# Products whose result nobody reads, put on TensorE before its first transposition and in four idle places

## The chip, the cores and the metric
One NeuronCore of one Trainium2 chip runs the kernel. The metric is the device time of one execution in microseconds (us), the median of several runs. Other executions than the profiled one carry no trace; durations below come from that single profiled execution.

## The reference, cut to what matters
The input x is 16 batches of 256 tokens of 128 features, float32. Two residual layers follow each other.

```
x = x + attention(layernorm(x))       # 16 heads, 16 query/key features, 8 value features a head
    q, k, v = x @ Wq, x @ Wk, x @ Wv;  q = q / 4
    A = (q . k)^2 under a causal mask;  o = (A v) / (sum of A + 1e-5);  o @ Wo
    # chunked in the reference with a running state; equal to one causal pass over 256 tokens
x = x + moe(layernorm(x))             # 8 experts, the last chosen of the best 2 writes the token
    scores = softmax(x @ gate_w + gate_b);  best two;  wi = score of the expert
    y = relu(x * wi @ w1[e] + b1[e]) @ w2[e] + b2[e]        # 128 -> 512 -> 128
```

Where both of a token's two experts write, the later one stands, so each token needs one expert only, and the kernel sorts tokens by that expert.

## The kernel before, in words
**Attention.** The work goes batch by batch, 16 batches, in `PERIODS`: in period p the scores belong to batch p-1, while projections of the next batch and the tail of earlier ones are laid between them. A batch's scores are made in four groups of four heads (`score_group(b, g)`, into the four banks of `sc`). ScalarE squares a group (`square`, line 416), which also frees `sc` for the next group; GpSimd masks it (`mask`, line 566); TensorE multiplies it by the values (`weigh`, into `av`). VectorE transposes and divides (`spread`, `divide`), TensorE applies Wo (`project_o`), VectorE adds the residual (`residual`) and chooses the expert (`route_*`). GpSimd sends each token's row to its expert's region in memory (`scatter`, line 594).

**Experts.** 39 tiles of 128 rows. For each tile TensorE runs `go_up` (eight recorded instructions into `sc`), a transposition of a later tile (`transpose_xw`), and `go_down` of the tile before (into `av` for even tiles, `p5` for odd ones). ScalarE makes the lower half of relu (`relu_low`, line 516), VectorE the upper half (`relu_high`, line 997) and the sum with the bias (`end_y`, line 1009). In the first ten tiles VectorE also works off `late_piece(t)`: the residual, the second normalisation and the routing of the last batches.

**Order.** Every engine's order is written out by hand; engines wait for one another by semaphores and run their own list strictly in order. On TensorE's list the start is: wait for `dve_const`, `transpose_xn(0)`, `centre_gate`, the first halves of the K and Q projections (`project_half`), `gate_output`, the second K half, and then `first_period`, which begins with `score_group(0, 0)`. The second K half waits for `half_k_ready[1]`, VectorE's copy of the first half (line 705). VectorE reaches that copy only after it has cleared `v_ext` (lines 685 to 692). GpSimd's constants come first of all: `ones` is one of its memsets (line 544), and `pool_step` becomes 1 with the iota of line 549. After the last period TensorE's list is: transposition of the biases, `project_o(14)`, `weigh(15, 2)`, the table load `experts(pe, 0)`, `weigh(15, 3)`, `transpose_xw(0)` and `(1)`, `go_up(0)`, `project_o(15)`, `transpose_xw(2)`, `go_up(1)`, `transpose_xw(3)`, `go_down(0)`, `prefix(6)`, `go_up(2)`.

All of TensorE's products are recorded under the helper's line 1068, transpositions under 1071. A float32 product is recorded as two instructions, a bfloat16 one as one.

Of the kernel before, what the change touches and what calls it, by code (L numbers as in the profile page):

```python
# [7 lines left out]
def after(engine, semaphore, count):  # L8

    if not (isinstance(count, int) and count <= 0):  # L10
        engine.wait_ge(semaphore, count)


def attention_moe_kernel(nc, x, Wq, Wk, Wv, Wo, gate_w, gate_b, w1, b1, w2, b2, out):
# [7 lines left out]
    NB, L, D = x.shape  # L22
    P = 128
    NTK = L // P
    H, F, HD = 16, 16, 8
    E, _, FF = w1.shape
# [49 lines left out]
    with ctx:  # L76
        def sb(name, shape, dt=fp32):
            return ctx.enter_context(nc.sbuf_tensor(name, shape, dt))

        def sem(name):  # L80
            return ctx.enter_context(nc.semaphore(name))
# [17 lines left out]
        ones = sb("ones", [P, P], bf16)  # L99
# [87 lines left out]
        sc = ctx.enter_context(nc.psum_tensor("sc", [P, GH, 512], fp32))  # L187
        av, p5, p6, p7 = [ctx.enter_context(nc.psum_tensor(n, [P, 512], fp32)) for n in ("av", "p5", "p6", "p7")]
# [16 lines left out]
        pool_step = sem("pool_step")  # L205
# [72 lines left out]
        def of(p, lag):  # L278
            return p - lag if 0 <= p - lag < NB else None

        def pair_of(p, lag):

            return (p - lag) // PAIR if 0 <= p - lag < NB and (p - lag) % PAIR == 0 else None
# [16 lines left out]
        def experts(engine, w):  # L300

            engine.wait_ge(table_ready[w], 1)
            words = loaded(engine, expert_i[w][0:1, :], E ** PACK - 1)
            return [(words[t // PACK] >> (BITS * (t % PACK))) & (E - 1) for t in range(LENGTH[w])]
# [761 lines left out]
        def _(pe):  # L1066
            def mm(o, l, r, start=True, stop=True):
                return nc.tensor.matmul(o, lhsT=l, rhs=r, start=start, stop=stop)  # L1068

            def transpose(o, i):  # L1070
                return nc.tensor.transpose(o, i, ident[:, :])  # L1071

            def score_group(b, g):


                if b == 0 and g == 0:
                    pe.wait_ge(half_q_ready, 1)
                if b == 0 and g < 2:
                    pe.wait_ge(half_k_ready[g], 1)
                if g == (2 if b == 0 else 0):  # L1080
                    pe.wait_ge(q_ready, b + 1)
                if b == 0 and g >= 2 or b > 0 and g < 2:
                    pe.wait_ge(k_ready[g % 2], b + 1)
                after(pe, squared, GROUPS * b + g)
                q, k, at = q_sb[b % 2], k_sb[b % 2][g % 2], (g // 2) * L
                for c in range(GH):
                    strip = slice(STRIP * c, STRIP * (c + 1))
                    mm(sc[:, c, P:SW], k[strip, at:at + P], q[strip, at:at + L])
                for c in range(GH):
                    strip = slice(STRIP * c, STRIP * (c + 1))  # L1090
                    last = mm(sc[:, c, 0:P], k[strip, at + P:at + L], q[strip, at + P:at + L])
                last.then_inc(scored, 1)

            def weigh(b, g):
                gg, r = g // 2, g % 2
                pe.wait_ge(masked, GROUPS * b + g + 1)
                if g == 0:
                    pe.wait_ge(v_ready, b + 1)
                    after(pe, u_ready, b)
                    if b == 0:  # L1100
                        pe.wait_ge(gate_made, 3)
                v, half = v_ext[b % 2], gg * L
                for c in range(GH):
                    mm(av[STRIP * c:STRIP * (c + 1), half:half + L], v[:, 0, r, GH * gg + c, :],
                       scores[g][:, c, 1:3, :], start=r == 0, stop=False)
                for c in range(GH):
                    last = mm(av[STRIP * c:STRIP * (c + 1), half + P:half + L], v[:, 1, r, GH * gg + c, :],
                              scores[g][:, c, 0, :], start=False, stop=r == 1)
                last.then_inc(av_done, 1)

            def transpose_xn(b):
                pe.wait_ge(xn_ready, b + 1)
                after(pe, q_ready, b)
                for j in range(NTK):
                    last = transpose(p6[:, j * P:(j + 1) * P], xn[b % 2][:, j, :])
                last.then_inc(tn_done, 1)

            def project_q(b):
                pe.wait_ge(xnT_ready, b + 1)
                for g in range(NG):  # L1120
                    last = mm(p6[:, g * L:(g + 1) * L], wq_sb[:, g * P:(g + 1) * P], xnT[b % 2][:, :])
                last.then_inc(q_done, 1)

            def project_k(b):
                after(pe, k_ready[1], b)
                for g in range(NG):
                    last = mm(p5[:, g * L:(g + 1) * L], wk_sb[:, g * P:(g + 1) * P], xnT[b % 2][:, :])
                last.then_inc(k_done, 1)
# [13 lines left out]
            def project_o(b):  # L1142
                pe.wait_ge(oT_ready, b + 1)

                after(pe, x2_ready, b)
                after(pe, raw_ready, min(b + 3, NB))
                after(pe, counts_read, min((b + LATE - CHOICE) // PAIR, NP - 3) + 1)
                if b == 0:
                    pe.wait_ge(gate_made, 3)
                for j in range(NTK):  # L1150
                    last = mm(projected[:, j, :], oT[:, j * P:(j + 1) * P], wo_sb[:, :])
                last.then_inc(wo_done, 1)
# [17 lines left out]
            def gate_output():  # L1170
                pe.wait_ge(gate_made, 2)
                mm(av[:, E:2 * E], woT[:, :], wv_sb[:, D:DE]).then_inc(gate_step, 1)


            pe.wait_ge(dve_const, 2)
            transpose_xn(0)
            centre_gate()
# [10 lines left out]
            def first_period():  # L1188
                score_group(0, 0)
                pe.wait_ge(half_q_ready, 1)  # L1190
                project_half(p6, wq_sb, 1, q_done)
                pe.wait_ge(wv_in, 16)
                project_v(0)
                score_group(0, 1)
                transpose_xn(1)
                score_group(0, 2)
                project_q(1)
                project_k(1)
                score_group(0, 3)
                project_v(1)  # L1200
                weigh(0, 0)
                weigh(0, 1)
                transpose_xn(2)

            for p in PERIODS:
                new, core, late, tail = of(p, 0), of(p, CORE), of(p, LATE), of(p, TAIL)
                nxt, choice = of(p, -1), pair_of(p, CHOICE)
                if core is None:
                    continue
                if core == 0:  # L1210
                    first_period()
                    continue
                score_group(core, 0)
                if tail is not None:
                    project_o(tail)
                if new is not None and new > 0:
                    project_q(new)
                score_group(core, 1)
                if late is not None:
                    weigh(late, 2)  # L1220
                    weigh(late, 3)
                score_group(core, 2)
                if new is not None and new > 0:
                    project_k(new)
                if choice is not None:
                    prefix(choice)
                if new is not None and new > 0:
                    project_v(new)
                if nxt is not None and nxt > 0:
                    transpose_xn(nxt)  # L1230
                score_group(core, 3)
                weigh(core, 0)
                weigh(core, 1)
# [36 lines left out]
            pe.wait_ge(left_ready, 1)  # L1270
            nc.tensor.transpose(xw_bank[:, 0:E * FC], b1_rows[:, :], ident[0:E * FC, 0:E * FC]).then_inc(b1_done, 1)
            project_o(NB - 2)
            weigh(NB - 1, 2)
            e = experts(pe, 0)
            weigh(NB - 1, 3)
            pe.wait_ge(b1_ready, 1)
            transpose_xw(0)
            transpose_xw(1)
            for t in range(TILES):
                go_up(t)  # L1280
                if t == WAVE:
                    e = e + experts(pe, 1)
                if t == 0:
                    project_o(NB - 1)
                if t + 2 < TILES:
                    transpose_xw(t + 2)
                if t:
                    go_down(t - 1, e[t - 1])
                if t == 1:
                    prefix(NP - 2)  # L1290
                if t == 6:
                    prefix(NP - 1)
# [24 lines left out]
```

## Time and profile before
| what | value |
|---|---|
| runs | 274.76 us median of 3 (274.31 to 275.97) |
| the profiled execution | 274.99 us, span 273.0 us |
| TensorE (PE) busy | 245.6 us, 90% |
| VectorE (DVE) busy | 195.5 us, 72% |
| ScalarE (ACT) busy | 169.9 us, 62% |
| GpSimd (POOL) busy | 166.0 us, 61% |
| mean granted TensorE clock | 0.989 |

The span goes from the first to the last instruction; 2.0 us of the execution lie outside it. A row of a timeline gives the start, the length from the start of the first to the end of the last instruction of the row, the engine, the line, what is written and read, how many instructions are merged (x8), and in brackets how long the engine was idle before and what released it. TensorE's instructions overlap: the next one starts before the modelled end of the one before, so the pace is read from start to start.

### The profile page before, as it was taken

Reading aid. Unit: us, or ns where it says so; the run is one execution under the profiler, and the core shown is the slowest. Engines: PE = TensorE matmul, PEld = TensorE weight load, DVE = VectorE, ACT = ScalarE, POOL = GpSimd, SP = SyncE. Lnnn points to the kernel's source line nnn. Section 1 sums busy time; section 2 is a strip of 40 time slices with the busy share of each in tenths; the row PEclk is TensorE's granted clock in tenths of the full one; section 3 lists DMA queues with packets and bytes.
Section 4 is the critical chain, followed back from the end, with each engine's and each line's share of the span. In section 5 each row is a group of like instructions: output and inputs, shape, how many; then the busy total and the mean of one; then the engine's idle time right before and its main releaser. Section 6 shows DMA issues by size and latency. Waiting matters only on the chain.

```text
span 273.0 us, 8984 instructions
## 1 busy us (share of the span) xinstructions
PE 245.6 (90%) x3045; PEld 199.5 (73%) x3045; DVE 195.5 (72%) x711; ACT 169.9 (62%) x315; POOL 166.0 (61%) x190
## 2 busy tenths in 40 slices
PE   0989999999999999999999999666998999999993
PEld 0666777777777767767767767435998999999993
DVE  4643466787799899899799798759878655555562
ACT  1386767767767767767777776544456556556550
POOL 6263364564786786786677667850477775455454
PEclk9999999999999999999999999998999999999998
DMA  5799999999600000000000000456666489777500
GB/s 152 227 342 353 352 356 352 352 335 357 196 25 22 2 22 21 2 23 22 2 20 23 2 22 20 116 134 175 185 166 169 119 241 283 180 211 178 150 29 9
DMA packets 31692, 40.57 MB, mean 149 GB/s; under 512 B 3442, under 2 KB 24468, under 8 KB 31648
## 3 DMA queue, kind: packets, MB, share of 16 engines
q1 hardware_dynamic: 29120, 35.69, 43.9%
q0 software_dynamic: 2272, 4.25, 4.5%
q8 instruction: 25, 0.41, 0.7%
q14 instruction: 19, 0.16, 0.2%
q10 hardware_dynamic: 256, 0.07, 0.1%
HBM read 17.98 MB, written 22.48 MB: 148 GB/s over the span
## 4 chain that ended last, share of the span: by engine, by line
PE 69%; ACT 16%; POOL 5%; issue 4%; DVE 3%; DMA 1%; SPq 0%; DVEq 0%; ACTq 0%; POOLq 0%
PE sc L1068 33%; PE p L1068 24%; ACT scores L416 16%; PE av L1068 9%; PE p L1071 3%; POOL expert_rows L594 2%; POOL scores L566 2%; DMA rows<-in_L_attn_hidden_states 1%; POOL out L607 1%; DVE scaled L768 0%; POOL rstd L583 0%; DVE logit L770 0%; DVEq L296 0%; DVE u_sb L718 0%; DVE xn L662 0%
## 5 line engine op out<-in xcount | busy, mean ns | idle before, releaser
L416 ACT ACTIVATE scores<-sc 128x1536 f32<-128x1536 f32 x64 | 92.8, 1451 | 47.0 <-PE sc L1068 47.0
L566 POOL TENSOR_SCALAR_AFFINE_SELECT scores<-scores 128x1024 f32<-128x1024 f32 x64 | 71.3, 1115 | 47.7 <-ACT scores L416 47.1
L1068 PE MATMUL sc<-q_sb,k_sb 32*128 32x256 f32 (+1 forms) x1024 | 60.9, 350 | 10.9 <-ACT scores L416 7.4
L1068 PEld LDWEIGHTS sc<-q_sb,k_sb 32*128 32x128 f32 x1024 | 48.5, 186 | 28.5 <-issue 18.3
L607 POOL DMA_INDIRECT out<-y_sb,xr x39 | 38.4, 983 | 27.6 <-DVE y_sb L1009 22.5
L1068 PE MATMUL av<-scores,v_ext 128*32 128x256 f32 (+1 forms) x1024 | 48.7, 329 | 0.9 <-POOL scores L566 0.9
L516 ACT ACTIVATE hT<-sc,b_sb 128x128 f32<-128x128 f32 x78 | 24.6, 364 | 35.7 <-PE sc L1068 34.9
L1068 PE MATMUL sc<-xwT,w_t 128*128 128x128 f32 x312 | 42.0, 279 | 0.0
L1068 PEld LDWEIGHTS av<-scores,v_ext 128*32 128x32 f32 x1024 | 28.8, 110 | 16.2 <-POOL scores L566 1.4
L997 DVE TENSOR_SCALAR hT<-sc,b_sb 128x128 f32<-128x128 f32 x78 | 23.8, 347 | 21.6 <-PE sc L1068 18.4
L594 POOL DMA_INDIRECT expert_rows<-rows,slot_i x32 | 32.8, 1024 | 10.7 <-issue 7.3
L1068 PEld LDWEIGHTS sc<-xwT,w_t 128*128 128x128 f32 x312 | 38.4, 194 | 0.0
L1068 PE MATMUL av<-w_sb,hT 128*128 x160 | 23.6, 293 | 0.7 <-ACT hT L516 0.4
L1068 PEld LDWEIGHTS av<-w_sb,hT 128*128 128x128 f32 x160 | 20.2, 198 | 3.1 <-issue 2.2
L1068 PE MATMUL p<-w_sb,hT 128*128 x152 | 21.2, 282 | 0.8 <-ACT hT L516 0.8
L509 ACT ACTIVATE xw<-xr 128x128 f32<-128x128 f32 x39 | 19.8, 509 | 0.6 <-issue 0.6
L1068 PEld LDWEIGHTS p<-w_sb,hT 128*128 128x128 f32 x152 | 18.4, 191 | 2.2 <-issue 1.4
L1068 PE MATMUL p<-xnT,wk_sb 128*128 128x256 f32 x64 | 19.3, 423 | 0.0
L718 DVE STREAM_TRANSPOSE u_sb<-av 128x512 f32<-128x512 f32 x16 | 11.4, 713 | 9.8 <-PE av L1068 9.8
L1068 PE MATMUL p<-xnT,wq_sb 128*128 128x256 f32 x64 | 17.9, 401 | 0.0
L700 DVE TENSOR_SCALAR k_sb<-p,parity 128x512 f32<-128x512 f32 x15 | 11.1, 740 | 7.4 <-ACT k_sb L439 7.4
L662 DVE TENSOR_SCALAR xn<-rows,mv,rstd 128x128 f32<-128x128 f32 x32 | 15.1, 513 | 0.0
(136 smaller groups left out, 322.9 us busy)
## 6 DMA issues: line engine op xcount, KB each, us to landing
expert_rows<-pad_rows SPq DMA_DIRECT2D x11, 1572.0 KB, 18.3
w_t<-in_L_ffn_w SPq DMA_DIRECT2D x39, 256.0 KB, 3.5
xr<-expert_rows SPq DMA_DIRECT2D x39, 65.5 KB, 2.7
rows<-in_L_attn_hidden_states SPq DMA_DIRECT2D x16, 128.0 KB, 3.2
out<-y_sb,xr POOLq DMA_INDIRECT x39, 3.0
b_sb<-in_L_ffn_b SPq DMA_DIRECT2D x1, 512.0 KB, 5.8
expert_rows<-rows,slot_i POOLq DMA_INDIRECT x32, 2.4
wo_sb<-in_L_attn_Wo ACTq DMA_DIRECT2D x8, 8.0 KB, 2.4
```

The source lines that it names most:

```text
L416: nc.scalar.activation(scores[g][:, :, :, :].rearrange("p c a t -> p c (a t)"), sc[:, :, 0:SW], ACT.Square, scale=Q_SCALE).then_inc(square ...
L509: nc.scalar.activation(xw[t % 2][:, :], xr[t % XR][:, 0:D], ACT.Identity, bias=xr[t % XR][:, MEAN:MEAN + 1], scale=xr[t % XR][:, FACTOR:FA ...
L516: ins = nc.scalar.activation(hT[t % 2][:, c * P:(c + 1) * P], up_bank[t % 2][0][:, c * P:(c + 1) * P], ACT.Relu, bias=b1_sb[:, bass.ds(e * ...
L566: nc.gpsimd.affine_select(out=scores[g][:, :, 0:2, :], in_=scores[g][:, :, 0:2, :], compare_op=ALU.is_ge, fill=0.0, base=0, pattern=[[0, G ...
L594: nc.gpsimd.indirect_dma_start(out=region, out_offset=bass.IndirectOffsetOnAxis(ap=slot_i[:, b, j:j + 1], axis=0), in_=rows[:, b, j, :], i ...
L607: nc.gpsimd.indirect_dma_start(out=out.rearrange("b l d -> (b l) d"), out_offset=bass.IndirectOffsetOnAxis(ap=xr[t % XR][:, IDCOL:IDCOL + ...
L662: ins = nc.vector.tensor_scalar(xn[b % 2][:, j, :], rows[:, b, j, 0:D], mv1[:, b, j, 0:1], rstd1[:, b, j:j + 1], ALU.subtract, ALU.mult)
L700: nc.vector.tensor_scalar(k_sb[b % 2][1][:, :], p5[:, :], parity[:, 1:2], None, ALU.mult).then_inc(k_ready[1], 1)
L718: nc.vector.transpose(u_sb[:, :, :, :, :].rearrange("p n g r w -> p g n (r w)"), av[:, :].rearrange("p (g n w) -> p g n w", g=NG, w=STRIP) ...
L997: ins = nc.vector.tensor_scalar(hT[t % 2][:, c * P:(c + 1) * P], up_bank[t % 2][1][:, at:at + P], b1_sb[:, bass.ds(e * FC + c, 1)], 0.0, A ...
L1068: return nc.tensor.matmul(o, lhsT=l, rhs=r, start=start, stop=stop)
L1071: return nc.tensor.transpose(o, i, ident[:, :])
```

## The change
A function `stay_busy(n, bank)` issues n products of a 128x128 bfloat16 matrix of ones with 512 bfloat16 columns of the same ones. Their results go into a bank that nobody reads before it is written again. It is called in five places of TensorE's list: 11 products ahead of the first transposition, after a wait for `pool_step`; 5 ahead of `score_group(15, 3)`; 3 between `project_o(14)` and `weigh(15, 2)`; 5 between `weigh(15, 3)` and `transpose_xw(0)`; 6 between `go_up(0)` and `project_o(15)`. Nothing is removed or moved.

```diff
+            def stay_busy(n, bank):
+
+                for _ in range(n):
+                    mm(bank, ones[:, :], ones[:, :].unsqueeze(1).broadcast_to([P, 4, P]))
+
+
+            pe.wait_ge(pool_step, 1)
+            stay_busy(11, sc[:, 0, :])
             pe.wait_ge(dve_const, 2)
             transpose_xn(0)
             centre_gate()
...
                     transpose_xn(nxt)
+                if p == NB:
+
+                    stay_busy(5, p5[:, :])
                 score_group(core, 3)
...
             project_o(NB - 2)
+            stay_busy(3, p5[:, :])
             weigh(NB - 1, 2)
             e = experts(pe, 0)
             weigh(NB - 1, 3)
+            stay_busy(5, p5[:, :])
             pe.wait_ge(b1_ready, 1)
             transpose_xw(0)
             transpose_xw(1)
...
                 if t == 0:
+                    stay_busy(6, p5[:, :])
                     project_o(NB - 1)
```

## Rows read from the trace of the kernel before

**Rows 1.** The page: chain that ended last, by engine; granted clock in 40 slices.
```profile
PE 69%; ACT 16%; POOL 5%; issue 4%; DVE 3%; DMA 1%; SPq 0%; DVEq 0%; ACTq 0%; POOLq 0%
PEclk9999999999999999999999999998999999999998
```
**Rows 2.** Windows: length, busy us (instructions) of PE, PEld, DVE, ACT, POOL, granted clock, DMA.
```profile
188.50:189.00 0.50, 0.50 (x5) 0.50 (x4) 0.47 (x4) 0.50 (x2) 0.00 (x0) 0.50 0.72 124
...
191.50:192.00 0.50, 0.50 (x6) 0.48 (x5) 0.37 (x2) 0.00 (x0) 0.42 (x2) 0.59 0.59 131
```
**Rows 3.** Timeline of PE, 6 to 21 us: start, length, instruction, count.
```profile
6.53 0.66 PE L1071 MATMUL p<-ident,xn 128*128 128x128 f32 x2 [6.53 <-DVE xn L662]
...
10.17 1.22 PE L1068 MATMUL p<-xnT,wk_sb 128*128 128x256 f32 x2
11.32 1.67 PE L1068 MATMUL sc<-q_sb,k_sb 32*128 32x256 f32 x16
...
14.73 0.94 PE L1068 MATMUL sc<-q_sb,k_sb 32*128 32x256 f32 x16
...
19.16 1.03 PE L1068 MATMUL p<-xnT,wk_sb 128*128 128x256 f32 x4
20.11 0.94 PE L1068 MATMUL sc<-q_sb,k_sb 32*128 32x256 f32 x16
```
**Rows 4.** Timelines of POOL, DVE and ACT, 1 to 16 us.
```profile
1.49 0.13 POOL L549 IOTA parity_i<- 128x1 int32 x1
...
8.95 0.12 DVE L692 MEMSET v_ext<- 128x16 f32 x3
9.63 0.48 DVE L705 TENSOR_SCALAR k_sb<-p,parity 128x256 f32<-128x256 f32 x1 [0.55 <-ACT k_sb L453]
...
9.04 0.47 ACT L453 ACTIVATE k_sb<-p,parity 128x256 f32<-128x256 f32 x1 [1.38 <-PE p L1068]
...
13.11 1.45 ACT L416 ACTIVATE scores<-sc 128x1536 f32<-128x1536 f32 x1 [2.59 <-PE sc L1068]
...
15.73 1.45 ACT L416 ACTIVATE scores<-sc 128x1536 f32<-128x1536 f32 x1 [0.54 <-PE sc L1068]
```
**Rows 5.** Timeline of PE, 176 to 191 us.
```profile
176.40 0.94 PE L1068 MATMUL sc<-q_sb,k_sb 32*128 32x256 f32 x16 [1.57 <-ACT scores L416]
...
180.30 0.86 PE L1068 MATMUL av<-scores,v_ext 128*32 128x256 f32 x16 [0.69 <-POOL scores L566]
...
183.43 0.30 PE L1071 MATMUL p<-ident,xw 128*128 128x128 f32 x1 [1.19 <-ACT xw L509]
...
184.31 1.12 PE L1068 MATMUL sc<-xwT,w_t 128*128 128x128 f32 x8
187.51 0.73 PE L1068 MATMUL p<-wo_sb,oT 128*128 128x136 f32 x4 [2.08 <-DVE oT L734]
...
188.19 1.63 PE L1068 MATMUL sc<-xwT,w_t 128*128 128x128 f32 x8
...
190.14 1.99 PE L1068 MATMUL av<-w_sb,hT 128*128 x8
```
**Rows 6.** The same timeline, 191 to 196 us.
```profile
191.99 0.26 PE L1068 MATMUL p<-onehot,ones 128*128 128x40 bf16 x4
192.09 1.14 PE L1068 MATMUL sc<-xwT,w_t 128*128 128x128 f32 x8
...
195.42 1.15 PE L1068 MATMUL av<-w_sb,hT 128*128 x8
```
**Rows 7.** Timeline of DVE, 189 to 193 us.
```profile
189.18 0.61 DVE L997 TENSOR_SCALAR hT<-sc,b_sb 128x128 f32<-128x128 f32 x2
...
191.26 0.61 DVE L997 TENSOR_SCALAR hT<-sc,b_sb 128x128 f32<-128x128 f32 x2
192.16 0.29 DVE L1009 TENSOR_TENSOR y_sb<-av,y_sb 128x128 f32<-128x128 f32 x1 [0.29 <-PE av L1068]
```
**Rows 8.** Windows with DVE's load beside PE's, columns as in rows 2.
```profile
196.00:198.00 2.00, 2.00 (x21) 2.00 (x20) 1.82 (x6) 0.94 (x5) 1.45 (x2) 1.00 0.52 165
```

## The prediction

> **What bounds the kernel now.** Begin with the chain of waits on the page [rows 1]: 69% of it is TensorE and 16% ScalarE, so a product made quicker is worth something wherever TensorE ends last, and nothing elsewhere. Next, the granted clock. The slices show one dip. The windows cut it out [rows 2]: 0.50 at 188.5 to 189.0 us and still 0.59 over 191.5 to 192.0. So TensorE ran at the lower of its two levels (1.2 instead of 2.4 GHz) for about 3.4 us. Ahead of the fall it was mostly idle: waits of 1.19 us before 183.43 and of 2.08 us before 187.51 [rows 5].
>
> The clock column shows no dip at the start, but the durations do. The 16 instructions of a score group took 1.67 us at 11.32 and 0.94 at 14.73; the second K half, two instructions, took 1.22 us at 10.17, where later four of them took 0.95 from start to start (19.16 to 20.11) [rows 3]. The same doubling stands under the dip: the up-projection took 1.63 us at 188.19 and 1.14 at 192.09 [rows 5, 6]. I read 6.5 to about 14 us as a second stretch at 1.2 GHz that the column doesn't show. Two stretches are therefore to be priced: which of their extra time lies on the path that sets the end?
>
> **The eleven products at the start.** They may begin when line 549 is done, at 1.62 us [rows 4], say 1.75. No row has 512 columns in bfloat16. The nearest of the same type is the 40-column product, four of which start within 0.10 us (191.99 to 192.09) [rows 6]: 0.025 us for 40 columns, which scaled by columns gives 0.32 us at the high clock and 0.64 at the low. That is the upper end, since a fixed part is scaled with it. The nearest by array time is a float32 instruction of 256 columns, 0.95/4 = 0.24 us [rows 3]. One column per cycle is the lower end: 512/2.4 GHz = 0.21, 512/1.2 GHz = 0.43. I take the lower end, because 0.24 for the big float32 instruction shows that long ones have little fixed time. Eleven at the low clock are then 4.7 us and end at 6.45, just ahead of the first transposition at 6.53 [rows 3], which waits for VectorE anyway: cost nothing. If the cover fails, they cost what they exceed it by; at 0.64 each they end at 8.8.
>
> The Trainium skill, "TensorE: Matmul & The Clock Gate", section "Wait — 56ns, not 53.3ns?", measures 0.427 us cold and 0.216 us warm from start to start for 512 columns; by it the eleven end at 6.45 too.
>
> **What a high clock is worth at the start.** Follow the first chain. The second K half starts at 10.17, released by VectorE's copy at 9.63 to 10.11 [rows 3, 4]. That copy waited 0.55 us for ScalarE's at 9.04, which waited for the first K half. With a warm TensorE that K half alone, a twin of the one at 10.17, takes at least 0.5 us less, and the transpositions before it shrink too; but VectorE clears v_ext until 9.07 [rows 4] and can't copy before about 9.15. So of what TensorE saves up to here only 9.63 - 9.15 = 0.48 us arrives. From there on TensorE alone sets the path. The K half from its start to that of the scores: 11.32 - 10.17 = 1.15 us, warm 0.95/2 = 0.48, saved 0.67. The scores to the start of ScalarE's square: 13.11 - 11.32 = 1.79, warm 15.73 - 14.73 = 1.00 [rows 3, 4], saved 0.79. The sum is 0.48 + 0.67 + 0.79 = 1.94 us at the first square. The next group's scores started at 14.73, 0.17 after that square's end at 14.56, so they are released by it, and the cold Q half and V projection that stand between the two groups on TensorE's list shrink into its shadow. I deduct 0.05: 1.9 us. From here the attention is a chain of squares and products without an outside clock to hold it, and shifts whole. Input rows come early enough: nothing after the first two statistics waits for them.
>
> **The nineteen later products.** At the high clock 0.21 each, bounds 0.21 to 0.32. Five (1.1, at most 1.6) lie in the 1.57 us wait before 176.40; three (0.64, at most 0.96) in the 0.69 us before 180.30; five (1.1, at most 1.6) in the 1.19 before 183.43; six (1.3, at most 1.9) in the 2.08 before 187.51 [rows 5]. All fit; at the upper bound the second and third stick out by 0.3 and 0.4 us. Behind them are queued weigh and a transposition, whose users have their own slack: VectorE is working off routing until 189. I take no cost.
>
> **What they give back.** With the clock held, the up-projection at 188.19 takes 1.1 instead of 1.63 and the down-projection at 190.14 takes 1.15 instead of 1.99 [rows 5, 6]: with the transposition between them 1.5 us of TensorE. Here I don't count it all. VectorE's upper half of relu for the first tile starts only at 189.18 and for the second at 191.26, with no idle time before either, though its input was there at 185.4 and 189.8 [rows 7, 5]. It waits for TensorE once, 0.29 us at 192.16. After that VectorE is the busy one in the first ten tiles, 1.82 of 2.00 us in the window shown [rows 8]. So 1.5 us of TensorE become 0.29 us of the end, with 0 and 1.5 as the ends of the range.
>
> **The sum.** 1.9 + 0.3 = 2.2 us. The profiled execution took 274.99 (span 273.0), so 272.8; it stood 0.23 above the median of the runs, 274.76, from which the same sum gives 272.6. I say 272.7, 0.8% less. What a measurement of this kernel can tell from no change is about 1%, 2.7 us: the limits are 272.0 and 277.5.
>
> **Rival 1, the clock doesn't come in time or doesn't stay.** The engine had worked from 6.53 for over 7 us before the scores got quick [rows 3]; the fillers begin only 4.8 us ahead of 6.53. They are denser, which speaks for them, but a warm start also halves the work between 6.5 and 10, leaving waits in which the clock may fall, as it did after the waits of rows 5. If the high clock is missing for the K half and the first scores, 1.46 of the 1.9 go, and 0.7 us or less in all remain, 274.1 to 274.8: 274.3. The Trainium skill, same page, section "What's actually happening", says that the gate's count runs free of the kernel's start, so that the rise comes at another point in each run; by it some executions get the 1.9 us and others nothing, and a median between them would be near this rival in part. The spread of the runs before, 1.66 us, fits that but doesn't show it. Chance 0.22.
>
> **Rival 2, VectorE isn't the limit of the early tiles.** If its late pieces can slide back while TensorE runs ahead, the whole 1.5 us arrive: 1.9 + 1.5 = 3.4, or 271.4. For: VectorE is idle for 0.18 of 2.00 us in the window of rows 8. Against: the relu starts of rows 7 follow VectorE's own work. Chance 0.14.
>
> **Rival 3, slower.** The first transposition stands behind the eleven products. The point from which this decides is (6.53 - 1.75)/11 = 0.435 us apiece, hardly over the 0.43 that I took. If the clock stays low all along and each takes 0.50, as the float32 instruction doubled would, they end at 7.25, everything starts 0.7 us later and nothing is saved: 275.7; at 0.64 it is 277.3. Chance 0.09.
>
> The products failing to alter the clock at all, with no delay either, is inside rival 1 (274.8).
>
> **Chances.** Forecast 0.55 with its own range 272.0 to 273.5; the rivals as given. The range 271.2 to 274.9 leaves out rival 3 and the ends of the others. Faster by over 1%: rival 2 and a tenth of the rest, 0.24. Slower by over 1% needs the upper price of rival 3 and more: 0.03. Within 1%: 0.73.
>
> **What would show it.** In the changed trace: eleven products from about 1.75 us, the later ones 0.21 apart; the first transposition still at 6.53; the second K half at 9.7 and four-instruction pace there; the first square at about 11.2 instead of 13.11, and the last one 1.9 us earlier too, at 175.5; granted clock 1.00 through 186 to 192; the upper relu of the second tile with no more gain than 0.3 us over that shift. The prediction is wrong if the first square moves by less than 1 us, if the shift shrinks between it and the last square, or if the tiles up to the tenth gain more than 0.5 us on their own.

## The result and the profile after

The changed kernel takes 270.99 us (median of 4 runs, 270.71 to 271.61), the kernel before beside it 275.07 (4 runs, 274.31 to 275.97). The ratio on record is 0.9868, 95% interval 0.9838 to 0.9899: faster by 1.3%. Here and below the ratios are those of the record; they are not the quotients of the medians, which can differ from them by up to 0.0034 (here the quotient is 0.9852), but lie in the same intervals. 272.7 was forecast, 271.2 to 274.9 the range: the median lies 0.2 us below its lower end. The profiled execution took 271.61 us (span 269.9), 3.4 less than that of before, of which 3.1 are in the span and 0.3 outside it. The direction was right. The gain was larger than the 2.2 us of the forecast's sum: by 0.9 in the spans, by nearly 2 between the medians (4.1 us).

The page after, busy time and chain by engine:

```profile
PE 249.5 (92%) x3075; PEld 198.8 (74%) x3075; DVE 195.2 (72%) x711; ACT 169.8 (63%) x315; POOL 165.8 (61%) x190
...
PE 67%; ACT 17%; POOL 5%; issue 4%; DVE 4%; DMA 1%; SPq 0%; DVEq 0%; ACTq 0%; POOLq 0%
```

TensorE is busy 3.9 us longer in a shorter span; the chain hardly changes. The timeline of PE at the start, against [rows 3]:

```profile
1.67 4.76 PE L1068 MATMUL sc<-ones 128*128 128x512 bf16 x11 [1.67 <-POOL parity_i L549]
6.51 0.41 PE L1071 MATMUL p<-ident,xn 128*128 128x128 f32 x2
...
9.64 0.70 PE L1068 MATMUL p<-xnT,wk_sb 128*128 128x256 f32 x2 [0.32 <-DVE k_sb L705]
10.27 0.94 PE L1068 MATMUL sc<-q_sb,k_sb 32*128 32x256 f32 x16
...
12.93 0.94 PE L1068 MATMUL sc<-q_sb,k_sb 32*128 32x256 f32 x16 [0.64 <-ACT scores L416]
```

The eleven end at 6.43, the transposition stands at 6.51, and from there every product has its quick length: 0.94 us for the first scores, which took 1.67. The second K half now waits for VectorE. That wait and the first square, from the timelines of DVE and ACT, against [rows 4]:

```profile
8.90 0.16 DVE L692 MEMSET v_ext<- 128x16 f32 x4
9.10 0.48 DVE L705 TENSOR_SCALAR k_sb<-p,parity 128x256 f32<-128x256 f32 x1
...
11.33 1.45 ACT L416 ACTIVATE scores<-sc 128x1536 f32<-128x1536 f32 x1 [1.81 <-PE sc L1068]
```

The end of the attention and the first tiles, timeline of PE, against [rows 5]:

```profile
172.78 1.25 PE L1068 MATMUL p<-ones 128*128 128x512 bf16 x5
174.42 0.94 PE L1068 MATMUL sc<-q_sb,k_sb 32*128 32x256 f32 x16 [0.39 <-ACT scores L416]
...
183.29 1.46 PE L1068 MATMUL p<-ones 128*128 128x512 bf16 x6
185.53 0.73 PE L1068 MATMUL p<-wo_sb,oT 128*128 128x136 f32 x4 [0.78 <-DVE oT L734]
...
186.21 1.06 PE L1068 MATMUL sc<-xwT,w_t 128*128 128x128 f32 x8
...
188.16 1.15 PE L1068 MATMUL av<-w_sb,hT 128*128 x8 [0.71 <-ACT hT L516]
```

The windows say 1.00 for the granted clock where it had been 0.50:

```profile
180.00:186.00 6.00, 4.77 (x37) 2.62 (x26) 4.55 (x16) 2.58 (x9) 0.00 (x0) 1.00 0.65 170
186.00:192.00 6.00, 5.29 (x50) 5.05 (x49) 5.33 (x27) 2.87 (x10) 1.27 (x2) 1.00 0.68 178
```

And VectorE in the first tiles, against [rows 7]:

```profile
187.19 0.61 DVE L997 TENSOR_SCALAR hT<-sc,b_sb 128x128 f32<-128x128 f32 x2
...
189.28 0.61 DVE L997 TENSOR_SCALAR hT<-sc,b_sb 128x128 f32<-128x128 f32 x2
189.80 0.28 DVE L1009 TENSOR_TENSOR y_sb<-av,y_sb 128x128 f32<-128x128 f32 x1
```

**Where the 3.1 us of the two spans went,** from the starts of the same groups and tiles in both traces. The second score group starts 1.80 us earlier (14.73 to 12.93), and this shift holds up to the 21st. By the 25th it is 1.99 (75.38 to 73.39): in the trace before, the 21st group took 1.21 us, and in the changed kernel it takes 0.94. So it is with three traces against eleven: 1.21 or 1.22 us wherever nothing is added at the start (the kernel before and two traces of the later products alone), 0.94 wherever products are added there, five, eleven or fourteen, and also where they have 8 columns and do nothing for the clock. So these 0.2 us come with the added instructions and not with the clock; why, no run shows. Timeline of PE, first before, then with 8 columns:

```profile
64.82 1.21 PE L1068 MATMUL sc<-q_sb,k_sb 32*128 32x256 f32 x16 [0.23 <-ACT scores L416]
...
63.83 0.94 PE L1068 MATMUL sc<-q_sb,k_sb 32*128 32x256 f32 x16 [0.23 <-ACT scores L416]
```

The shift is 1.98 at the second tile's up-projection (188.19 to 186.21) and 2.68 at the twelfth's (211.85 to 209.17): 0.70 gained in the early tiles. The last 0.4 arise in the remaining tiles. That stretch, from the twelfth up-projection to the last but one, took 51.97 us before and 51.55 after; four further traces with the same later products gave 51.1, 51.1, 51.1 and 52.1, so 0.4 is within the spread from trace to trace.

### The profile page after: what moved, and what is told of

Same layout as the page of the kernel before. It is cut to its first block, busy times and chain, and to the rows that moved or that the text cites. A ratio compares the mean times of both kernels' runs of the same rounds, so it can differ in the third digit from the quotient of the medians.

```text
span 269.9 us, 9044 instructions
## 1 busy us (share of the span) xinstructions
PE 249.5 (92%) x3075; PEld 198.8 (74%) x3075; DVE 195.2 (72%) x711; ACT 169.8 (63%) x315; POOL 165.8 (61%) x190
## 4 chain that ended last, share of the span: by engine, by line
PE 67%; ACT 17%; POOL 5%; issue 4%; DVE 4%; DMA 1%; SPq 0%; DVEq 0%; ACTq 0%; POOLq 0%
PE sc L1068 33%; PE p L1068 23%; ACT scores L416 17%; PE av L1068 8%; PE p L1071 3%; POOL expert_rows L594 2%; POOL scores L566 2%; DMA rows<-in_L_attn_hidden_states 1%; POOL out L607 1%; DVE scaled L768 0%; POOL rstd L583 0%; DVE logit L770 0%; DVEq L296 0%; DVE v_ext L687 0%; DVE v_ext L685 0%
## 5 line engine op out<-in xcount | busy, mean ns | idle before, releaser
L1068 PE MATMUL sc<-q_sb,k_sb 32*128 32x256 f32 (+1 forms) x1024 | 59.9, 347 | 10.3 <-ACT scores L416 6.8
L1068 PEld LDWEIGHTS sc<-q_sb,k_sb 32*128 32x128 f32 x1024 | 47.8, 184 | 27.8 <-issue 18.8
L1068 PE MATMUL sc<-xwT,w_t 128*128 128x128 f32 x312 | 41.4, 276 | 0.0
L1068 PE MATMUL av<-w_sb,hT 128*128 x160 | 22.8, 286 | 1.3 <-ACT hT L516 1.1
L1068 PEld LDWEIGHTS av<-w_sb,hT 128*128 128x128 f32 x160 | 19.4, 191 | 3.4 <-issue 2.3
L1068 PE MATMUL p<-xnT,wk_sb 128*128 128x256 f32 x64 | 18.2, 405 | 0.6 <-DVE k_sb L705 0.3
L1068 PE MATMUL p<-xnT,wq_sb 128*128 128x256 f32 x64 | 16.9, 384 | 0.0
L700 DVE TENSOR_SCALAR k_sb<-p,parity 128x512 f32<-128x512 f32 x15 | 11.1, 740 | 7.4 <-ACT k_sb L439 7.4
```

The lines of the kernel that those rows point to most:

```text
L700: nc.vector.tensor_scalar(k_sb[b % 2][1][:, :], p5[:, :], parity[:, 1:2], None, ALU.mult).then_inc(k_ready[1], 1)
```

## The experiments

Two chips were in play. On the first the kernel before takes 274 us; on the second it takes 294 to 295. In the traces of its variants there, engines stand still from about 85 us on, for input rows or for nothing that the profile shows. Each version has its ratio to the kernel before on the same chip. The repeat of the changed kernel, the later clearing, and the five and fourteen products ran on the first chip, all others on the second. The record doesn't name the chip of the main result; its times are those of the first. On the second the changed kernel as it stands was never run.

**Start alone.** The changed kernel without the nineteen later products.

```diff
-                    stay_busy(5, p5[:, :])
...
-            stay_busy(3, p5[:, :])
...
-            stay_busy(5, p5[:, :])
...
-                    stay_busy(6, p5[:, :])
```

> Only the eleven products ahead of the first transposition; the nineteen later ones are gone. Theory (the start gives the shift of 1.8 us to the first square, VectorE limits the early tiles): the first square starts at 11.3 us as in the changed kernel, the span is 1.8 to 2.0 us below the kernel before, ratio about 0.993. The clock may fall again near 186 us; if it does, that costs no more than 0.5 us of the end. Rival (TensorE limits the early tiles): if the clock falls there, the first up- and down-projections lose 1.5 us and all of it reaches the end, so that this kernel stands 1.5 us or more behind the changed one.

Measured: ratio 0.9944 (0.9906 to 0.9982), 292.48 against 293.94 us. The clock did what no theory of mine had: it rose in time, and fell again. Timeline of PE:

```profile
1.67 4.32 PE L1068 MATMUL sc<-ones 128*128 128x512 bf16 x11 [1.67 <-POOL parity_i L549]
...
15.18 1.37 PE L1068 MATMUL sc<-q_sb,k_sb 32*128 32x256 f32 x16 [1.28 <-ACT scores L416]
16.48 2.08 PE L1068 MATMUL p<-xnT,wq_sb 128*128 128x256 f32 x4
18.35 1.33 PE L1068 MATMUL p<-xnT,wk_sb 128*128 128x256 f32 x4
19.61 0.94 PE L1068 MATMUL sc<-q_sb,k_sb 32*128 32x256 f32 x16
```

The Q projection takes 2.08 us where it takes 1.13 warm, and the fourth score group starts at 19.61, not 18.30. The same kernel again:

> The kernel with the eleven products at the start alone, again, for a call on a chip on which the kernel before takes about 274 us. The five-product kernel (later products kept, start not in time) stood 0.9 us below the kernel before, the full one 3.1 us. Theory (the two parts add up): the start alone is worth 2.0 to 2.3 us, ratio 0.992; the trace shows a stretch of low clock between 183 and 195 us and the time from the first tile's upper relu to the tenth tile's down-projection is 0.5 to 0.7 us longer than with the later products. Rival (the later products are worth nothing of their own): ratio as the full change, 0.988.

Measured: ratio 0.9895 (0.9847 to 0.9943), 292.92 against 295.02 us. The interval holds the theory (0.992) and the rival (0.988). This time the trace has no fall at the start, the fourth group stands at 18.29. Without the later products a stretch of low clock lies at the end of the attention (the granted clock is the third column from the end):

```profile
178.00:184.00 6.00, 2.46 (x44) 1.83 (x34) 3.89 (x14) 2.46 (x2) 5.43 (x7) 0.79 0.64 197
184.00:190.00 6.00, 5.82 (x73) 3.49 (x73) 3.71 (x12) 2.63 (x5) 1.20 (x2) 0.64 0.46 118
190.00:196.00 6.00, 4.40 (x41) 3.62 (x34) 5.14 (x21) 3.38 (x11) 0.00 (x0) 1.00 0.67 165
```

It lies ahead of the tiles here, so the tile times I had announced can't be read from it.

**Later products alone.** The changed kernel without this line:

```diff
-            stay_busy(11, sc[:, 0, :])
```

> Only the nineteen later products; the eleven at the start are gone. Theory: the first square starts at 13.1 us as in the kernel before; no fall of the clock between 180 and 192 us; the second tile's upper relu stands as in the kernel before and the third's comes 0.3 to 0.5 us earlier, which is all that reaches the end: ratio 0.998 to 0.999. Rival: TensorE's whole 1.5 us reach the end, ratio 0.994 to 0.995. If the 0.4 us that the tiles from the tenth on gained in the changed kernel come from the later products, they appear here too and the ratio is 0.997.

Measured: ratio 0.9961 (0.9925 to 0.9997), 292.87 us. Repeated:

> The kernel with the nineteen later products alone, again, under the same condition. Theory: 0.5 to 0.9 us below the kernel before, ratio 0.997 to 0.998; first square near 13 us (between 11.9 and 13.2, depending on when the clock rises by itself), no low clock after 180 us. Rival (they are worth the whole 1.5 us of TensorE): ratio 0.9945.

Measured: ratio 0.996 (0.9933 to 0.9988), 294.33 against 295.02 us. Twice a ratio 0.4% below 1, by the medians 1.1 and 0.7 us: more than my theory's, less than the rival's. Each interval leaves room for both. On this chip the last score group starts about 8 us later than before on the first (184.18 and 184.74 against 176.40), and in the second trace the clock was low for a while before the later products began (0.72 over 178 to 184 us).

**The same products with 8 columns.**

```diff
-                    mm(bank, ones[:, :], ones[:, :].unsqueeze(1).broadcast_to([P, 4, P]))
+                    mm(bank[:, 0:8], ones[:, :], ones[:, 0:8])
```

> All thirty added products stand in the same places of TensorE's list, but have 8 columns in place of 512, so they hardly occupy the array. If the time comes from the clock, this kernel is like the kernel before: first square at 13.1 us, a fall of the clock near 188 us, ratio 0.999 to 1.001. If a part comes from another cause that the added instructions bring (a shift of TensorE's instruction stream, other gaps between the tiles), that part stays here: the 0.2 us gained near 65 us and the 0.4 us gained after the tenth tile would give a ratio of about 0.998.

Measured: ratio 1.0002 (0.9965 to 1.0038). Thirty more instructions in the same places that hardly occupy the array bring nothing that stands out of 0.4% of noise; the gain of 1.3% comes with the occupation. Only the 0.2 us of the 21st score group, named above, are in this trace too. Timeline of PE:

```profile
1.67 0.46 PE L1068 MATMUL sc<-ones 128*128 128x8 bf16 x11 [1.67 <-POOL parity_i L549]
6.29 0.66 PE L1071 MATMUL p<-ident,xn 128*128 128x128 f32 x2 [4.16 <-DVE xn L662]
...
9.94 1.22 PE L1068 MATMUL p<-xnT,wk_sb 128*128 128x256 f32 x2
11.09 0.94 PE L1068 MATMUL sc<-q_sb,k_sb 32*128 32x256 f32 x16
```

The K half is still slow at 9.94 and the scores are quick at 11.09; before, the scores of that place were slow. So the clock rises by itself at another point from execution to execution: between the K half and 11.1 us here, near 14 in the trace before, after the second score group's start at 14.7 in the five-product trace below.

**Seven more products after the second up-projection.**

```diff
+                if t == 1:
+                    stay_busy(7, p5[:, :])
                 if t + 2 < TILES:
```

> The changed kernel with seven more products of 512 columns right after the up-projection of the second tile, 1.5 us of TensorE at the high clock, the amount that the low clock had cost there. Theory (VectorE limits the early tiles): the down-projection of the first tile starts at about 188.8 instead of 188.2 us and the third tile's upper relu 0.1 to 0.5 us later, and the end by as much: ratio to the kernel before 0.988 to 0.990. Rival (TensorE limits them): all 1.5 us reach the end, ratio about 0.992 to 0.993.

> The changed kernel with seven more products after the second tile's up-projection, again, under the same condition. On the other chip the input rows came late, TensorE reached that up-projection after VectorE's first relu, and VectorE then waited 1.46 us for the first down-projection. Here the up-projection starts 1 us ahead of that relu. Theory (VectorE limits the early tiles, with 1.0 to 1.5 us of slack for TensorE at this place): VectorE waits 0.0 to 0.3 us for the first down-projection, the end moves by as much, ratio as the changed kernel's within 0.001 (0.987 to 0.989). Rival: 1.5 us later, ratio 0.993 to 0.994.

Measured: 0.9947 (0.9914 to 0.998) and 0.9951 (0.9923 to 0.9979), no changed kernel without the stall beside it. The traces speak against my theory for this chip. Timeline of DVE in the first:

```profile
193.22 0.61 DVE L997 TENSOR_SCALAR hT<-sc,b_sb 128x128 f32<-128x128 f32 x2
...
195.31 0.61 DVE L997 TENSOR_SCALAR hT<-sc,b_sb 128x128 f32<-128x128 f32 x2
197.38 0.29 DVE L1009 TENSOR_TENSOR y_sb<-av,y_sb 128x128 f32<-128x128 f32 x1 [1.46 <-PE av L1068]
```

VectorE waits 1.46 us for the first down-projection (0.89 in the second trace). From the second up-projection to the first down-projection it is 2.51 us in both traces, against 1.21 in both traces of the later products alone: 1.3 of the stall's 1.5 us arrive there. Whether they reach the end isn't shown, since from the second to the twelfth up-projection it is 32.0 and 33.0 us with the stall and 31.0 and 32.7 without. Here the second up-projection began at 193.77, 0.55 after VectorE's first relu; on the first chip it begins 0.98 us ahead of it (186.21 and 187.19). Both runs were on the second chip, so the stall was never measured where my argument was made.

**The changed kernel again, on the first chip.**

> The changed kernel once more, beside the others of this call. Where the clock rises ahead of the first transposition and does not fall again before the fourth score group, the first square starts at 11.3 us and the fourth score group at 18.3. In an execution in which it falls once after its rise (the kernel with the eleven products alone showed that: its fourth group started at 19.6 instead of 18.3) 1.3 us of the 1.8 are lost. If the gain of a run depends on this, the ratio lies between 0.987 and 0.993 and the runs of the changed kernel spread over 1 us and more.

Measured: 271.27 us (6 runs, 270.78 to 273.5), ratio 0.9885 (0.9837 to 0.9932) to 274.37. Its trace is one of an execution of 272.54 us, and has the fall. Timeline of PE, then windows:

```profile
1.67 4.24 PE L1068 MATMUL sc<-ones 128*128 128x512 bf16 x11 [1.67 <-POOL parity_i L549]
...
15.35 1.66 PE L1068 MATMUL sc<-q_sb,k_sb 32*128 32x256 f32 x16 [1.28 <-ACT scores L416]
16.94 2.02 PE L1068 MATMUL p<-xnT,wq_sb 128*128 128x256 f32 x4
```

```profile
15.00:15.50 0.50, 0.15 (x4) 0.18 (x5) 0.00 (x0) 0.50 (x3) 0.42 (x2) 0.86 1.02 377
15.50:16.00 0.50, 0.50 (x8) 0.47 (x12) 0.16 (x2) 0.31 (x2) 0.50 (x1) 0.50 1.07 397
18.50:19.00 0.50, 0.50 (x3) 0.41 (x2) 0.00 (x0) 0.02 (x1) 0.41 (x1) 0.72 1.05 385
```

Four of the six runs lie within 270.78 to 271.56, two at 272.54 and 273.5. The mean granted clock, which is on record for every run, tells them apart: 0.994 in the last two, of which one is the traced one with the fall, 0.996 to 1.000 in the other four. In the four runs of the main result it is 0.998 to 1.000, so none of them is likely to have had the fall: the 270.99 us are those of the undisturbed start, and that was luck of the draw. Ahead of the fall TensorE had waited 0.63 us before the second and 1.28 before the third score group.

**VectorE clears the second v_ext buffer later.**

```diff
-            nc.vector.memset(v_ext[1][:, :, :, :, :], 0.0).then_inc(dve_const, 1)
...
                     norm1_stats((2, 3), ln1_count(2))
+                    nc.vector.memset(v_ext[1][:, :, :, :, :], 0.0).then_inc(dve_const, 1)
+                    set_ones(1, 5)
```

> The changed kernel with VectorE's clearing of the second v_ext buffer moved behind its copy of the first K half and the next statistics. Theory (in the changed kernel only 0.5 of the start's 0.8 us arrive, because VectorE clears until 9.1 us): VectorE's copy starts at 8.75 instead of 9.10, the second K half at 9.3 instead of 9.64, the first square at 11.0 instead of 11.33, and 0.35 us of that reach the end. Rival: another wait takes its place at once (ScalarE's copy of woT, the second half of K on VectorE, which now follows the clearing), and the first square or the third score group stands where it stood.

Measured: VectorE's copy at 8.67, the first square at 10.90 (timelines of DVE and ACT):

```profile
8.67 0.48 DVE L707 TENSOR_SCALAR k_sb<-p,parity 128x256 f32<-128x256 f32 x1 [0.92 <-ACT k_sb L453]
...
10.90 1.45 ACT L416 ACTIVATE scores<-sc 128x1536 f32<-128x1536 f32 x1 [1.55 <-PE sc L1072]
```

Its first transposition stands at 6.34. Against the trace just shown, where that is 6.35, the K half starts at 9.21 instead of 9.47: 0.26 us, not 0.35, since the copy now waits for ScalarE. The clearing was what held it. In the medians it is not seen: 271.92 us (270.39 to 272.4), ratio 0.9893 (0.985 to 0.9937). Four of these six runs have a mean clock of 0.989 to 0.994, no higher than the run with the fall, and lie at 271.86 to 272.4; the two others took 270.39 and 270.7, against 270.78 to 271.56 for the changed kernel's four. That fits 0.26 us, on two runs.

**Five and fourteen products at the start.** The 11 of `stay_busy(11, ...)` becomes 5 or 14.

> The changed kernel with five products at the start in place of eleven; they end at about 3.8 us and TensorE then idles until 6.5. Theory (the clock must be up before the first transposition, and rose 4.5 us after the first product in the changed kernel): it is not up, the first square starts at about 13.0 us and the gain of the start is gone: 1.5 to 1.9 us more than the changed kernel in the same call. Rival (any early work wakes the clock): first square at 11.3 and no difference.

Measured: 273.46 us, ratio 0.9964 (0.9939 to 0.9989), 2.2 us more than the repeat of the changed kernel beside it (271.27). Timelines of PE and ACT:

```profile
1.67 2.31 PE L1068 MATMUL sc<-ones 128*128 128x512 bf16 x5 [1.67 <-POOL parity_i L549]
6.28 0.66 PE L1071 MATMUL p<-ident,xn 128*128 128x128 f32 x2 [2.30 <-DVE xn L662]
...
11.07 1.67 PE L1068 MATMUL sc<-q_sb,k_sb 32*128 32x256 f32 x16
...
14.73 1.55 PE L1068 MATMUL sc<-q_sb,k_sb 32*128 32x256 f32 x16
```

```profile
12.87 1.45 ACT L416 ACTIVATE scores<-sc 128x1536 f32<-128x1536 f32 x1 [2.59 <-PE sc L1068]
```

Five wake nothing: the first square comes at 12.87, as slowly as before, and the second score group is slow as well. What remains, 0.9 us below the kernel before, is the later products' part on this chip, with the 0.2 us of the 21st group in it.

> The changed kernel with fourteen products at the start in place of eleven. Theory (eleven just fit): at 0.21 us for each of the last ones the first transposition starts at 7.0 to 7.1 instead of 6.51 us if the clock has risen, and at 7.7 if it has not; the part of that which VectorE's clearing until 9.1 us does not hide reaches the first square: 0.1 to 0.5 us more than the changed kernel. Rival (it keeps the clock up longer or makes the rise surer): as quick as the changed kernel or quicker, with fewer low-clock products between 6.5 and 20 us.

Measured: 272.35 us, ratio 0.9911 (0.988 to 0.9943). The transposition starts at 7.27, close behind the fourteen, and the first square at 11.80, 0.47 after that of the changed kernel's first trace (11.33) and 0.63 after that of its repeat (11.17): the upper end of what I gave, or a little over. The median is 1.1 us above the repeat's 271.27, more than the 0.1 to 0.5 expected, with intervals that overlap.

```profile
1.67 5.76 PE L1068 MATMUL sc<-ones 128*128 128x512 bf16 x14 [1.67 <-POOL parity_i L549]
7.27 0.38 PE L1071 MATMUL p<-ident,xn 128*128 128x128 f32 x2
```

**Five more products in the wait ahead of the third score group,** on top of the later clearing.

```diff
                 transpose_xn(1)
+                pe.wait_ge(gate_made, 3)
+                stay_busy(5, av[:, :])
                 score_group(0, 2)
```

> The kernel that clears the second v_ext buffer later, with five more products in TensorE's wait ahead of the third score group (1.28 us in the changed kernel's trace), where in three traces the clock fell at the third score group and cost 1.4 us. Theory: no fall there in any execution; the first square at 11.0 to 11.1 us, the fourth score group at 17.9 to 18.0; the runs lie closer together than the changed kernel's and their median is 270.4 to 270.7, ratio 0.985. Rival (the falls are rare in the timed runs, or the five products delay the third score group): median 271.3 or more, no better than the changed kernel.

Measured: 291.98 us (6 runs, 291.54 to 293.29), ratio 0.9889 (0.9851 to 0.9928), beside 0.9895 for the second run of the start alone. Timeline of PE:

```profile
1.67 4.38 PE L1072 MATMUL sc<-ones 128*128 128x512 bf16 x11 [1.67 <-POOL parity_i L550]
...
13.55 1.24 PE L1072 MATMUL av<-ones 128*128 128x512 bf16 x5
14.99 0.94 PE L1072 MATMUL sc<-q_sb,k_sb 32*128 32x256 f32 x16 [0.21 <-ACT scores L416]
...
17.78 0.94 PE L1072 MATMUL sc<-q_sb,k_sb 32*128 32x256 f32 x16
```

The fourth group stands at 17.78 and the clock stays up. Look at the length of the eleven products in all traces: 4.76, 4.85 and 4.87 us where no fall followed; 4.32, 4.29, 4.24 and 4.04 where it did. Shorter means that more of them ran at the high clock, so the rise was earlier. With 4.38 this one belongs to the early ones and did not fall. It is one trace. The six runs spread over 1.75 us, the changed kernel's over 0.9 and 2.7. The absolute time can't be set beside the first chip's, and whether this version beats the changed kernel stays open.

## Why the prediction was right in sign and short in size

**The products' own price: right.** 0.43 us each at the low clock; eleven in 4.76 us, the last of them quicker. The end at 6.43 and the transposition at 6.51 are as foreseen. At the high clock they take the 0.21 that was given (five in 1.25 us, six in 1.46), and the transposition of the first tile moved with the rest (183.43 to 181.45), so the later ones cost nothing. The point from which rival 3 decides is real: fourteen cost 0.47 us at the first square. Eleven leave hardly any room, the less so since the first transposition can start as early as 6.11 us in other executions (a trace of the later products alone).

**The start, 1.9 us: right in the trace.** The three terms 0.48, 0.67 and 0.79 came out as 9.64 for the K half (0.53), 0.63 from it to the scores (0.52 saved) and 1.06 to the square (0.73 saved): 1.78. That VectorE's clearing swallows the rest was shown by moving it. The value against other executions differs, since the clock rises by itself at different points: 2.2 us between the five-product kernel and the changed one, and only 0.8 at the first square against the 8-column trace (12.15 to 11.33), where it rose early. The forecast took one execution's rise, near 14 us, for the kernel's; that the number came out is in part luck.

**Rival 1, the clock doesn't stay: partly true.** It falls again at the third score group in four of the seven traces with eleven products and nothing in that wait, and costs 1.6 us in three of them: from the third group's start to the fourth's it is 4.4 us instead of 2.8. In the fourth, down for twice as long, it is 5.3, and 0.6 more up to the next. The prediction looked for the fall between 6.5 and 10 us; it comes after the waits of 0.63 and 1.28 us. The second of them exists in the kernel before too (1.29 us before 17.33); the first comes with the quick start, as the rival said of other waits. How often it happens in the timed runs their mean clock suggests: none of the four of the main result, two of the six of the repeat. The Trainium skill, "TensorE: Matmul & The Clock Gate", section "What's actually happening", says that the gate's count runs free of the kernel, so that the rise shifts from run to run; that the rise shifts the traces bear out, with eleven identical products taking 4.04 to 4.87 us.

**The later products: the term that was mis-sized.** I gave 0.29 us, and named a gain of over 0.5 in the tiles up to the tenth as a sign of being wrong. That sign came. The trace shows 0.70 between the second and the twelfth up-projection, and 0.6 to 0.7 in four further traces (22.93 to 23.05 us against 23.66). The failing step is "it waits for TensorE once, 0.29 us at 192.16". The idle column leaves out that VectorE's next instruction starts before the one before it ends. From the second relu to the next instruction it is 191.26 to 192.16 = 0.90 us before and 189.28 to 189.80 = 0.52 after: 0.38, not 0.29. A second wait, for the next down-projection, had no idle entry at all: 0.64 from relu to sum before, 0.53 after, 0.11. Together with smaller ones VectorE's tenth relu comes 0.54 us earlier than the shift at the first (209.70 to 207.17, against 189.18 to 187.19). The other 0.16 arises on TensorE. The times say 1.0 to 1.2 us by the ratios (0.9961, 0.996 and 0.9964), with intervals that reach from 0.1 to 2.2, and 0.7 to 1.1 by the medians. What they hold beyond 0.7 isn't explained, except for 0.2 us of the last, the 21st score group.

**Rival 2, all 1.5 us: not so on the first chip.** 0.7 of 1.5 arrived, and the two traces show which. The slow second up-projection cost nothing: TensorE, freed of the low clock, now idles 0.71 us ahead of the first down-projection, which starts 0.35 us after the end of VectorE's first relu before (189.79 and 190.14) and 0.36 after (187.80 and 188.16). The profile names ScalarE for that wait, but its relu of that moment is the second tile's, and the down-projection of the first doesn't need it; the first tile's began at 183.72. Timeline of ACT after:

```profile
187.53 0.62 ACT L516 ACTIVATE hT<-sc,b_sb 128x128 f32<-128x128 f32 x2 [0.47 <-PE sc L1068]
```

The slow down-projection arrived whole at first: from it to the third up-projection it is 1.95 us before (190.14 to 192.09) and 1.11 after (188.16 to 189.27), so TensorE's shift grows from 1.98 to 2.82. VectorE's follows only to 2.51 at its fourth relu and stays there through the eleventh, and TensorE's falls back to it, 2.52 at the ninth up-projection. That reads as VectorE holding the pace of the early tiles, but it is read from two traces and not shown by an experiment; the chain that ended last runs through TensorE there and doesn't show it. The experiment for it, seven more products, ran only on the other chip, where the slack was not there.

**Other causes:** with 8 columns nothing remains that stands out of the noise, so the added instructions and their places account for no more than a part: the 0.2 us of the 21st group, which the prediction had no term for. The last 0.4 us of the span, after the twelfth tile, are within the spread of traces.

## What to carry to other kernels

In this kernel products that nobody reads paid where TensorE would idle anyway and the next products were on the path; their number is bounded by the idle time at the low clock, and the clock can drop again in a later stretch with waits, so those want the same look. Where a trace's clock column shows nothing, compare the same shape at two times. Read the slack of a busy engine from start to start, not from its idle entries, and don't take one execution's clock for the kernel's.

## What the runs showed of the hardware

Eleven products of ones times ones in bfloat16 with 512 columns, begun at 1.67 us, had the first K half at its high-clock length in all eight traces (0.67 us against 1.18 to 1.19); eleven with 8 columns, or five with 512, did not. The kernel's own work, begun at 6.1 to 6.5 us, brought the clock up at about 11 to 16 us. It fell in a stretch in which TensorE had waited 0.63 and 1.28 us, in four of seven traces with the same start. The moment of the rise differs between executions of one kernel. The second chip ran the same kernel 7% slower (294 against 274 us). In the traces the instruction lengths are the same, 0.94 us for a score group; the time is in gaps, such as this one inside a score group of the start-alone kernel, where one weight load came late, at 86.84 us (timeline of PE):

```profile
85.72 0.93 PE L1068 MATMUL sc<-q_sb,k_sb 32*128 32x256 f32 x15 [0.23 <-ACT scores L416]
86.87 0.34 PE L1068 MATMUL sc<-q_sb,k_sb 32*128 32x128 f32 x1 [0.21 <-issue]
```
